# Scatters of normed rows spread over a group, in a kernel of attention and a mixture of experts

## The chip, the cores and the metric

One core of one Trainium2 chip runs the kernel. The metric is the device time of one execution in microseconds. Before the change the median of three runs is 1402.72 us (1402.52 to 1405.96).

## The reference

The input x is 64 sequences of 128 tokens of width 256, float32. Cross attention with 16 heads of 16 is followed by a mixture of 8 experts, of which each token takes two.

```
x = x + attention(layernorm(x), ctx, ctx; Wq,bq,Wk,bk,Wv,bv,Wo,bo)   # 16 heads, softmax over 128 keys
y = layernorm(x)
probs = softmax(y @ router)            # 8 experts
w, idx = top_k(probs, 2); w = softmax(w)
x = x + sum over the 2 chosen e of w_e * (silu(y @ gating[e]) * (y @ up[e])) @ down[e]
```

## The kernel before, in words

**Two parts.** Part one runs over 16 groups (g) of 4 sequences (b = 0 to 3, i = 4g+b). One turn of i is called a stage here. The attention of a sequence is spread over several stages, and beside it the same stages norm the attention's result (x1), choose each token's experts and write the normed rows, sorted by expert, to a table `sorted_x` in device memory. Part two (FFN) takes units of 256 or 128 rows of that table, all of one expert, and adds each result row to the output.

**The order of TensorE in a stage** (`stage_a` of the tensor block) is written out by hand: `scores(i)` (L527, 32 matmul records over 32 rows and 128 columns), `project(i-2)` and `values` or `queries` (L498, 4 records each), `attend(i-1)` (L552, 32 short records), `swap_max(i)` (L533), a product of keys or queries with 512 columns (L498, 4 records) or, in b = 3, the values of the next group, then four swaps of 128 columns (L504 or L568), in b = 0 the router's product (L576, 16 short records), in b = 2 the places (14 tiny products), and `scores_swapped(i)` (L541, 32 short records), after which the next stage's `scores` follow. A float32 product is two matmul records, each with its weight load (PEld).

**What the rows' scatters are.** `write_rows(g, ...)` (L425) on GpSimd (POOL) issues eight indirect DMAs for group g: for each of the 4 sequences and each of the 2 chosen experts, 128 rows of 261 floats go from `xn2` to the rows that `slots_now` names. In the kernel before, group g-3 is written in group g: four scatters in b = 0 and four in b = 1, in the program's order; they follow `route_rows(g-3)` of VectorE (DVE), which computes the slots in b = 0 between `row_maxes` (L1004) and `take_max_off` (L1011). Nothing but the slots' semaphore holds them, so the eight leave one behind the other. In the FFN the last three groups are written behind tiles 0 and 1, 10 and 11, 16 and 17; there `write_pads` (L466) writes the pads and `add_unit` (L459) adds result rows, all by indirect DMAs.

**What else POOL does in a group:** `root2(g-1)` (L411) in b = 1 behind the scatters, `keep_x(g+1)` (L418) behind it and behind the scores of b = 2, `root(g+2)` (L407) in b = 3.

**Buffers and counts.** `xn2` has two rooms of normed rows (g % 2) and `slots_now` one. `second_norm(g)` of ScalarE (ACT) in b = 2 writes a room and waits until the rows of group g-2 have landed; the last step of `route_rows` waits until the rows of group g-1 have landed. All scatters count on one semaphore, `s_scat`.

**SyncE (SP)** loads x and ctx for group g+2 and a block of expert weights (512 KB each), stores x1, and spreads the keys and queries of sequence i+1 over 32-row strips (`spread`, L280). The queries' spread of b = 3 is behind the ctx load in SP's program and needs the last queries product of that stage.

## Time and profile before

| | |
|---|---|
| median of three runs | 1402.72 us |
| the profiled execution | 1408.98 us |
| its span, first to last instruction | 1407.2 us |
| mean granted TensorE clock | 0.943 |
| TensorE busy (matmul) | 1308.4 us, 93% |
| VectorE, ScalarE, GpSimd busy | 645.9, 560.0, 422.8 us |
| scatters of rows L425 | 128, 124.1 us busy on POOL |

[...] Part one ends at about 676 us of the span.

### The profile page before, as it was taken

The page shows a single profiled execution, that of the slowest core. Times are in us where ns is not written, and L with a number is a line of the kernel's source. Part 1 is how long each engine was busy: PE and PEld are TensorE (multiplying, and loading weights), DVE is VectorE, ACT ScalarE, POOL GpSimd, SP SyncE. Part 2 cuts the span into 40 slices and gives each one's busy share as a digit, 9 for nine tenths or more (in the row PEclk, how much of TensorE's full clock was granted, in tenths as well). Part 3 has the DMA queues.
Part 4 walks back from the last instruction along what each step waited for, and adds up shares of the span by engine and source line. Part 5 has one row for each costly group of instructions (what it writes and reads, how often), then busy time and mean ns, then how long its engine had stood idle before and what let it go on. Part 6 is the DMA issues. An engine that isn't in the chain of part 4 may idle for free.

```text
span 1407.2 us, 30663 instructions
## 1 busy us (share of the span) xinstructions
PE 1308.4 (93%) x11214; PEld 1046.7 (74%) x11215; DVE 645.9 (46%) x1762; ACT 560.0 (40%) x924; POOL 422.8 (30%) x354
## 2 busy tenths in 40 slices
PE   6998898888999888997899899999999999999996
PEld 3676666666666666665688788888888888888996
DVE  3775675555675555665433533233232332323332
ACT  3564554444554444543454132222322223222352
POOL 3112322332313323212324632323323223232332
PEclk9998998888988888987999999999999999999999
DMA  4444333334333333222244443333434334343342
GB/s 129 129 114 129 115 114 109 113 103 121 117 116 112 114 101 88 86 62 77 59 64 74 94 61 50 53 49 53 53 49 53 49 53 53 48 54 46 49 52 34
DMA packets 171586, 112.44 MB, mean 80 GB/s; under 512 B 103345, under 2 KB 158641, under 8 KB 171473
## 3 DMA queue, kind: packets, MB, share of 16 engines
q1 hardware_dynamic: 143984, 72.75, 21.2%
q0 software_dynamic: 26400, 37.09, 15.3%
q8 instruction: 76, 1.25, 0.4%
q10 hardware_dynamic: 1088, 1.05, 0.2%
q14 instruction: 38, 0.30, 0.1%
HBM read 48.59 MB, written 45.46 MB: 67 GB/s over the span
## 4 chain that ended last, share of the span: by engine, by line
PE 86%; issue 6%; DVE 3%; DMA 2%; ACT 1%; another core or an unknown queue 1%; SPq 0%; POOL 0%; ACTq 0%; POOLq 0%; DVEq 0%
PE banks L498 65%; PE banks L527 9%; PE banks L541 5%; PE banks L552 4%; DMA heads<-qT 1%; PE banks L533 1%; PE banks L504 1%; DVE row_max L1004 1%; PE banks L568 1%; DMA out<-x_sb,token 1%; PE banks L576 1%; DMA ctxT_sb<-in_ctx 0%; DVE att_rows L1017 0%; DVE q_less L1011 0%
## 5 line engine op out<-in xcount | busy, mean ns | idle before, releaser
L459 POOL DMA_INDIRECT out<-x_sb,token x135 | 210.3, 1558 | 470.8 <-DVE x_sb L1322 413.3
L849 ACT ACTIVATE qT<-banks 128x1024 f32<-128x1024 f32 (+1 forms) x75 | 70.3, 938 | 485.4 <-PE banks L498 437.8
L1309 DVE TENSOR_TENSOR heads<-qT,banks 128x1024 f32<-128x1024 f32 (+1 forms) x75 | 83.5, 1113 | 358.6 <-PE banks L498 338.5
L498 PE MATMUL banks<-down_sb,heads 128*128 x1080 | 245.7, 379 | 0.9 <-DVE x_sb L1322 0.9
L498 PE MATMUL banks<-xnT,probs 128*128 128x256 f32 (+1 forms) x1184 | 240.8, 360 | 5.9 <-issue 5.7
L498 PE MATMUL banks<-xnT,kT 128*128 128x256 f32 (+1 forms) x1216 | 242.7, 357 | 0.0
L1004 DVE TENSOR_REDUCE row_max<-banks 128x16 f32<-128x2048 f32 x64 | 146.7, 2292 | 191.8 <-PE banks L527 191.7
L498 PEld LDWEIGHTS banks<-xnT,probs 128*128 128x128 f32 x1184 | 207.7, 190 | 33.8 <-issue 9.2
L498 PEld LDWEIGHTS banks<-xnT,kT 128*128 128x128 f32 x1216 | 211.8, 190 | 25.5 <-issue 0.4
L498 PEld LDWEIGHTS banks<-down_sb,heads 128*128 128x128 f32 x1080 | 203.7, 190 | 28.9 <-issue 1.9
L843 ACT ACTIVATE probs<-banks 128x512 f32<-128x512 f32 (+1 forms) x192 | 128.1, 740 | 136.6 <-remote 109.3
L527 PE MATMUL banks<-heads 32*128 32x128 f32 x2048 | 130.9, 313 | 54.0 <-issue 46.9
L425 POOL DMA_INDIRECT sorted_x<-xn,slots_now x128 | 124.1, 970 | 145.3 <-DVE slots_now L1103 86.3
L527 PEld LDWEIGHTS banks<-heads 32*128 32x128 f32 x2048 | 100.1, 203 | 82.0 <-issue 78.7
L1322 DVE TENSOR_SCALAR x_sb<-banks,weight 128x256 f32<-128x256 f32 x135 | 59.8, 480 | 121.4 <-PE banks L498 115.6
L541 PE MATMUL banks<-q_less,heads 32*128 32x128 f32 x2048 | 82.6, 289 | 3.4 <-issue 2.9
L498 PE MATMUL banks<-wo_sb,attnT 128*128 128x256 f32 x256 | 84.7, 459 | 0.9 <-DVE attnT L1032 0.7
L552 PEld LDWEIGHTS banks<-probs,v_aug 128*32 128x32 f32 x2048 | 55.2, 115 | 33.9 <-issue 33.1
L541 PEld LDWEIGHTS banks<-q_less,heads 32*128 32x128 f32 x2048 | 67.8, 190 | 16.3 <-issue 14.9
L498 PE MATMUL banks<-wv_sb,ctxT_sb 128*128 128x256 f32 x256 | 76.8, 429 | 0.4 <-ACT probs L843 0.4
L552 PE MATMUL banks<-probs,v_aug 128*32 128x128 f32 x2048 | 73.8, 288 | 3.1 <-ACT probs L843 3.1
L498 PE MATMUL banks<-ctxT_sb,wk_sb 128*128 128x512 f32 x128 | 63.1, 619 | 8.6 <-DMA ctxT_sb<-in_ctx 7.9
(165 smaller groups left out, 1286.1 us busy)
## 6 DMA issues: line engine op xcount, KB each, us to landing
xn<-sorted_x SPq DMA_DIRECT2D x240, 64.0 KB
x_sb<-in_x SPq DMA_DIRECT2D x16, 512.0 KB, 3.8
ctxT_sb<-in_ctx SPq DMA_DIRECT2D x16, 512.0 KB, 4.1
heads<-kT SPq DMA_DIRECT2D x128, 64.0 KB, 2.0
heads<-qT SPq DMA_DIRECT2D x128, 64.0 KB, 2.0
out<-x SPq DMA_DIRECT2D x16, 512.0 KB
gate_sb<-_L_ffn_kernel_gating_EDF SPq DMA_DIRECT2D x8, 512.0 KB
up_sb<-in_L_ffn_kernel_up_EDF SPq DMA_DIRECT2D x8, 512.0 KB
```

Of the source, the lines that this page charges most:

```text
L425: pool.indirect_dma_start(out=sorted_x[:, :], out_offset=bass.IndirectOffsetOnAxis(ap=slots_now[:, i:i + 1], axis=0), in_=xn2[:, u, i % GR ...
L459: pool.indirect_dma_start(out=out[:, :], out_offset=bass.IndirectOffsetOnAxis(ap=token[:, v, h:h + 1], axis=0), in_=ys[:, 2 * u + h, :], i ...
L498: last = nc.tensor.matmul(dst, lhsT, rhs, start=(i == 0), stop=(i == len(pairs) - 1))
L504: last = nc.tensor.transpose(bank[:, b * P:(b + 1) * P], xn[:, b, c * P:(c + 1) * P], ident[:])
L527: last = nc.tensor.matmul(score_banks(i)[:, j, c * TOK:(c + 1) * TOK], q_heads[strip(j), i % 2, c, :], k_heads[strip(j), i % 2, c, :], sta ...
L541: last = nc.tensor.matmul(score_banks(i)[:, j, c * TOK:(c + 1) * TOK], k_heads[strip(j), i % 2, c, :], q_less[strip(j), c, :], start=True, ...
L552: last = nc.tensor.matmul(bank[32 * j:32 * j + 32, q * TOK:(q + 1) * TOK], v_aug[:, i % 3, 4 * q + j, :], probs[:, j, c, :], start=True, s ...
L843: nc.scalar.activation(probs[:, j:j + n].rearrange("p j h t -> p j (h t)"), score_banks(i)[:, j:j + n], ACT.Exp, scale=DK ** -0.5).then_in ...
L849: nc.scalar.activation(gatedT[:, 0:w * F], gate_up[:, 0:w * F], ACT.Silu).then_inc(s_silu, 1)
L1004: nc.vector.reduce_max(row_max[:].rearrange("p (j r a) -> p j r a", r=16, a=2)[:, :, 0:4, 1], score_banks(i).rearrange("p j (h t) -> p j h ...
L1309: nc.vector.tensor_tensor(fusedT[:, u, 0:w * F], gatedT[:, 0:w * F], gate_up[:, 1024:1024 + w * F], ALU.mult).then_inc(s_fuse, 1)
L1322: last = nc.vector.tensor_scalar(ys[:, 2 * u + h, :], work[:, 0, h * D:(h + 1) * D], weight[:, v, h:h + 1], None, ALU.mult)
```

## The change

`xn2` gets three rooms (g % 3), `slots_now` two (g % 2), and the semaphore of the rows becomes one for each room. Group g's scatters are spread over the stages of group g+3 and one of them over b = 0 of g+4, each held by a semaphore of TensorE's: behind "scores of i done" or behind "attend(i-1) done". `keep_x` moves from the end of POOL's b = 1 to the start of its b = 2. `route_rows(g-3)` moves on VectorE from before `take_max_off` to behind `turn_attn` of b = 0. The waits for landed rows are for g-3 (rooms) and g-2 (slots). In the FFN two scatters more (the last two of group 12) stand behind tile 0.

```
+ROOMS = 3
-        xn2 = sb("xn2", [P, 2, GROUP, ROW])
+        xn2 = sb("xn2", [P, ROOMS, GROUP, ROW])
-        slots_now = sb("slots_now", [P, 2 * GROUP], u32)
+        slots_now = sb("slots_now", [P, 2, 2 * GROUP], u32)
+        s_rows_out = [sem(f"rows_written_room{r}") for r in range(ROOMS)]
+        def wait_rows(eng, g):
+            eng.wait_ge(s_rows_out[g % ROOMS], (g // ROOMS + 1) * 2 * GROUP * 16)
...
-            def write_rows(g, u, half, part=(0, GROUP)):
+            def write_rows(g, part):
                 wait(pool, s_route, g * ROUTE_STEPS + ROUTE_STEPS)
                 pool.nop(nofuse=True)
-                for i in range(GROUP * half + part[0], GROUP * half + part[1]):
+                for i in part:
                     pool.indirect_dma_start(
-                        out=sorted_x[:, :], out_offset=bass.IndirectOffsetOnAxis(ap=slots_now[:, i:i + 1], axis=0),
-                        in_=xn2[:, u, i % GROUP, :], in_offset=None).then_inc(s_scat, 16)
+                        out=sorted_x[:, :], out_offset=bass.IndirectOffsetOnAxis(ap=slots_now[:, g % 2, i:i + 1], axis=0),
+                        in_=xn2[:, g % ROOMS, i % GROUP, :], in_offset=None).then_inc(s_rows_out[g % ROOMS], 16)
...
             def stage_a(g, u, core, prev, prev2, prev3, nxt, far):      # POOL
                 for b in range(GROUP):
+                    i = g * GROUP + b
+                    if b == 2 and nxt:
+                        keep_x(g + 1, 1 - u)
+                    if g >= 3:
+                        pool.wait_ge(s_score, i + 1)
+                        if b == 0 and g >= 4:
+                            write_rows(g - 4, (6,))
+                        if b == 1:
+                            write_rows(g - 3, (0, 1))
+                        if b == 3:
+                            write_rows(g - 3, (4,))
+                        pool.wait_ge(s_att, i)
+                        if b == 0 and g >= 4:
+                            write_rows(g - 4, (7,))
+                        if b == 1:
+                            write_rows(g - 3, (2,))
+                        if b == 2:
+                            write_rows(g - 3, (3,))
+                        if b == 3:
+                            write_rows(g - 3, (5,))
+                    if b == 1 and prev:
+                        root2(g - 1)
                     if b == 3 and far:
                         root(g + 2)
-                    if b == 0 and prev3:
-                        write_rows(g - 3, 1 - u, 0)
-                    if b == 1:
-                        if prev3:
-                            write_rows(g - 3, 1 - u, 1)
-                        if prev:
-                            root2(g - 1)
-                        if nxt:
-                            keep_x(g + 1, 1 - u)
...
             def behind_tile(t):                                          # POOL, FFN
+                if t == 0:
+                    write_rows(GROUPS - 4, (6, 7))
...
-            def second_norm(g, u, pieces):
+            def second_norm(g, pieces):
                 wait(act, s_shift2, g + 1)
-                if not isinstance(g, int) or g > 1:
-                    wait(act, s_scat, BLANKS * 16 + (g - 1) * 2 * GROUP * 16)
-                normalise(xn2[:, u], x1, rstd2, shift2, pieces, s_norm2, cut=True)
+                if g >= ROOMS:
+                    wait_rows(act, g - ROOMS)
+                normalise(xn2[:, g % ROOMS], x1, rstd2, shift2, pieces, s_norm2, cut=True)
...
-                if not isinstance(g, int) or g > 0:
-                    wait(dve, s_scat, BLANKS * 16 + g * 2 * GROUP * 16)
-                steps.done(nc.vector.tensor_copy(slots_now[:], slot_f[:]))
+                if g >= 2:
+                    wait_rows(dve, g - 2)
+                steps.done(nc.vector.tensor_copy(slots_now[:, g % 2], slot_f[:]))
...
                     if b == 3 and far:                                   # DVE, stage_a
                         first_stats(g + 2, (2, 3))
-                    if b == 0 and prev3:
-                        route_rows(g - 3, 1 - u)
...
                     if one:
                         turn_attn(i - 1)
+                    if b == 0 and prev3:
+                        route_rows(g - 3)
```

## Rows read from the trace of the kernel before

**Rows 1.** The page: span, busy time of the engines, busy tenths in 40 slices.

```profile
PE 1308.4 (93%) x11214; PEld 1046.7 (74%) x11215; DVE 645.9 (46%) x1762; ACT 560.0 (40%) x924; POOL 422.8 (30%) x354
PEclk9998998888988888987999999999999999999999
```

**Rows 2.** Windows (length; PE, PEld, DVE, ACT, POOL busy; clock; DMA): group 2; last, group 3's b=3.

```profile
86.28:94.21 7.93, 7.93 (x130) 5.75 (x131) 5.13 (x9) 5.99 (x14) 0.00 (x0) 1.00 0.38 101
94.21:101.98 7.77, 7.74 (x115) 5.60 (x116) 6.63 (x21) 4.58 (x11) 1.01 (x1) 1.00 0.34 104
...
109.92:118.62 8.70, 7.81 (x114) 5.39 (x115) 6.94 (x20) 5.75 (x13) 1.02 (x1) 1.00 0.40 105
...
152.68:160.39 7.71, 7.71 (x114) 5.40 (x115) 6.94 (x19) 4.75 (x12) 1.02 (x1) 1.00 0.39 104
```

**Rows 3.** The same windows for b = 0 of the 13 groups 3 to 15.

```profile
118.62:135.45 16.83, 13.06 (x130) 8.91 (x130) 5.97 (x16) 5.01 (x12) 7.82 (x8) 0.78 0.34 105
...
sum 217.99, PE 164.39 PEld 112.18 DVE 78.07 ACT 71.27 POOL 100.88; mean PE 12.65 PEld 8.63 DVE 6.01 ACT 5.48 POOL 7.76
```

**Rows 4.** The same for b = 1 of these 13 groups.

```profile
135.45:144.74 9.29, 9.21 (x115) 6.69 (x116) 6.64 (x21) 4.61 (x11) 1.04 (x1) 0.85 0.29 88
177.19:187.62 10.43, 10.40 (x115) 7.28 (x116) 6.63 (x21) 4.56 (x11) 1.04 (x1) 0.74 0.25 78
...
sum 128.43, PE 127.15 PEld 90.37 DVE 87.74 ACT 58.02 POOL 13.53; mean PE 9.78 PEld 6.95 DVE 6.75 ACT 4.46 POOL 1.04
```

**Rows 5.** POOL's timeline in group 3 (start, length, what, idle before).

```profile
123.17 1.08 POOL L425 DMA_INDIRECT sorted_x<-xn,slots_now  x1 [6.29 <-DVE slots_now L1103]
...
132.17 0.96 POOL L425 DMA_INDIRECT sorted_x<-xn,slots_now  x1 [0.30 <-issue]
142.05 1.04 POOL L411 TENSOR_TENSOR rstd<-var_eps,minus_half 128x4 f32<-128x4 f32 x1 [8.93 <-DVE var_eps L995]
144.87 2.36 POOL L418 TENSOR_TENSOR x_bo<-x_sb,bo_sb 128x1024 f32<-128x1024 f32 x1 [1.78 <-PE banks L527]
```

**Rows 6.** DMA from 120 to 140 us, GB/s in 40 slices of 0.5 us.

```profile
GB/s 29 55 158 379 363 72 0 0 33 167 92 8 267 16 109 159 0 267 0 100 167 0 259 8 67 201 0 251 17 0 0 70 76 117 131 102 29 0 305 350
```

**Rows 7.** PE's timeline of group 3 beside the scatters.

```profile
124.42 1.29 PE L541 MATMUL banks<-q_less,heads 32*128 32x128 f32 x31
...
128.91 1.09 PE L527 MATMUL banks<-heads 32*128 32x128 f32 x5 [0.94 <-issue]
...
134.63 0.78 PE L527 MATMUL banks<-heads 32*128 32x128 f32 x2 [0.35 <-issue]
```

**Rows 8.** Timeline of group 2, without scatters.

```profile
97.29 1.88 PE L498 MATMUL banks<-ctxT_sb,wk_sb 128*128 128x512 f32 x4
...
100.75 1.17 PE L527 MATMUL banks<-heads 32*128 32x128 f32 x32
```

**Rows 9.** Windows: the stretch at the lower clock in group 3.

```profile
128.10:138.30 10.20, 7.47 (x27) 5.54 (x28) 2.63 (x3) 2.00 (x3) 3.84 (x4) 0.50 0.28 91
```

**Rows 10.** Timeline of the FFN: PE and POOL where 20 indirect DMAs follow closely.

```profile
784.01 0.99 POOL L425 DMA_INDIRECT sorted_x<-xn,slots_now  x1 [0.30 <-issue]
...
788.45 7.07 PE L498 MATMUL banks<-xnT,kT 128*128 128x256 f32 x32
...
800.37 1.91 PE L498 MATMUL banks<-xnT,probs 128*128 128x256 f32 x6 [1.40 <-issue]
802.60 1.12 PE L498 MATMUL banks<-xnT,probs 128*128 128x256 f32 x4 [0.33 <-issue]
804.03 1.11 PE L498 MATMUL banks<-xnT,probs 128*128 128x256 f32 x4 [0.31 <-issue]
```

**Rows 11.** The chain of waits at the end of group 2 (start, length, what).

```profile
113.88 3.37 DMA heads<-qT
```

**Rows 12.** Timeline of b = 0 of group 3: VectorE and the swap.

```profile
121.17 0.17 DVE L1093 TENSOR_SCALAR total<-gap 128x4 f32<-128x4 f32 x1
...
122.20 0.74 DVE L1011 TENSOR_TENSOR q_less<-heads,banks 128x256 f32<-128x256 f32 x2
...
123.31 0.60 PE L504 MATMUL banks<-ident,xn 128*128 128x128 f32 x4
```

91 lines of the change are left out of this document (47 added, 44 removed).

## The prediction

> **What bounds the kernel now.** I read the page first, then the timeline around the scatters, then windows cut from one row maximum to the next (one stage each), then the chain. The page says that TensorE is busy 93% of the span [rows 1], which seems to leave nothing. But a busy TensorE can be a slow one: its granted clock is 9 tenths or more in the slices of the FFN and falls to 8 or 7 in many of part one [rows 1]. The windows show where. Group 2, which writes no rows yet, has its b = 0 and b = 1 in 7.93 and 7.77 us, TensorE busy throughout at clock 1.00 [rows 2]. In the 13 groups that write rows, b = 0 takes 217.99 us together, 16.8 each [rows 3], and b = 1 128.43, some 9.9 each [rows 4]. The number of matmul records of the two is the same as in group 2 (130 and 115), so this is no added work of TensorE.
>
> The timeline says what it is. Eight scatters leave POOL from 123.17 to 133.13, one each 1.27 us [rows 5]. DMA traffic of theirs begins 1.3 to 1.8 us behind the first issue and ends by 134.5 [rows 6]. Beside it the scores product L527, which needs 1.17 us for 32 records without scatters [rows 8], comes in handfuls with "issue" idle time between, until 135.4 [rows 7]: TensorE waits for no semaphore, its instructions come late. [...]
>
> The FFN shows the same thing beside longer products. POOL issues 20 indirect DMAs from 784.01 on. TensorE's 256-column records go at full pace (32 in 7.07) until 798.97, then they too come in fours: one batch at 802.60, the next at 804.03, 1.43 us apart [rows 10]. So I take it thus: while scatters are in flight TensorE is fed some 4 records with their loads in 1.43 us, and it lives on a store of instructions. Size of the store: from 785.5 (issue plus 1.5) to 798.97 it ran 13.5 / 0.22 = 61 records (0.22 = 7.07 / 32) and was fed 13.5 / 1.43 x 4 = 38, so the store held about 23. A 512-column record takes 1.88 / 4 = 0.45 us or so [rows 8], 3 in 1.43 us: such a product does not need the store at all. The short ones use 39 in that time.
>
> **Ceiling.** Removing all the excess: b = 0, 217.99 - 13 x 7.93 = 114.9; b = 1, 128.43 - 13 x 7.77 = 27.4; together 142.3 us [rows 2 to 4]. The profiled execution took 1408.98 us (span 1407.2, 1.8 around it), so 1266.7. It stands 6.3 us above the median of 1402.72; for the median the ceiling is 1260.4. As that difference is small beside 142.3, the excess is there in unprofiled runs too, and no matter of the recording.
>
> **The change part by part.** Time is counted from the end of a stage's scores; behind it come two products (to 1.9), attend (to 2.9), the row maximum's swap, the 512-column product (to 4.9), swaps of 128 columns, scores_swapped and the next scores, to 7.8 or so. A scatter starts 0.9 us behind its releaser (slots ready at 122.28, POOL at 123.17 [rows 5, 12]) and its traffic some 1.5 behind that.
>
> Held by the scores (number 6 in b = 0, 0 and 1 in b = 1, 4 in b = 3): traffic from 2.4, beside the row maximum's swap and the long product. The long product keeps its pace; what is left is attend's tail and the swap, whose instruction may come late. Ends: 0, and 1.10, what a scatter costs in today's b = 0 (114.9 / 104). I take 0.3, near the long products' row.
>
> Held by attend (7 in b = 0, 2 in b = 1, 3 in b = 2, 5 in b = 3): released at 2.9, traffic from 5.3. That is not the long product, it is scores_swapped and the next scores, 64 short records. One pause of 1.43 us [rows 10] against a store of some 23 short records at 0.037 us (0.9 us) leaves 0.5. Ends again 0 and 1.10. The first train bears it out: beside its first two scatters L541 ran 31 records in 1.29 us [rows 7], against 1.17 for 32 short ones undisturbed [rows 8], the full stops came later.
>
> In b = 1 three follow closely (2.4, 3.7, 5.3): a lean stretch of some 4.3 us, in which 12 records are fed; the swaps, the long product and the xn swaps take about 10 of them, so scores_swapped finds the store nearly empty. I take 1.3 for the three, ends 0 and 3.3.
>
> In b = 3 the queries' spread is a chain of its own: in group 2 the scores waited for that DMA, 3.37 us, behind the ctx load [rows 11], and the stage took 8.70 instead of 7.71 [rows 2]. Two scatters now move data beside it: ends 0 and 1.0, I take 0.2 here.
>
> Sum per group: b = 0, 0.3 + 0.5; b = 1, 1.3; b = 2, 0.5; b = 3, 0.3 + 0.5 + 0.2; 3.6 us. Group 3 has no b = 0 part: 2.8. So 12 x 3.6 + 2.8 = 46.0. With all at the low ends 0; with all scatters at today's price 102 x 1.10 + 13 = 125.
>
> The clock: stalls of under 1.5 us with dense work between are what group 2's own 0.99 us wait was, and the clock stayed 1.00 there [rows 2]. I take 27.4 as saved whole.
>
> At nothing I put: route_rows behind turn_attn (today it delays the subtraction to 122.20, yet the xn swap starts at 123.31 right behind the long product [rows 12]; VectorE is busy 5.13 of the 7.93 us of a b = 0 without it [rows 2], and the idle rest holds its 1.1 us; if that cover is gone the next row maximum starts up to 1.1 us late). The waits for rooms and slots: rows land 2 us behind issue and are waited for two or more stages later. keep_x: today it already starts with the scores of b = 2, at 144.87, not with the end of b = 1 [rows 5]; SP's load of x hangs on it and stays. root2 is behind scatter 2 in POOL's order, over by 4.8; its input comes at about 6.5 (8.93 us of idle before 142.05 [rows 5]). root: input later still. Behind POOL's new waits stand only these. The two scatters more behind tile 0 lie beside records that kept full pace for 13 us [rows 10]; ends 0 and 2.2.
>
> [...]
>
> [...]
>
> **Sum.** 1266.7 + 46.0 = 1312.7 in the profile's terms, less 6.3: 1306.4. I forecast 1306.
>
> **Rivals.**
> 1. The store covers a lone scatter whole. For it: the first two of the train cost next to nothing [rows 7]. Against: the pause, 1.43, is longer than the store lasts with short products. Cost 0 to 1.3 a group, so 1260 to 1277; say 1270. Chance 0.17.
> 2. A scatter costs the same wherever it is, and only the clock comes back: 104 scatters at 1.10 are kept. 1402.7 - 27.4 = 1375. Against: FFN products at full pace [rows 10]. Chance 0.08.
> 3. [...] Group 2 has the same loads and stores without the loss, so 0.02.
> 4. Slower: the clock. Today one train costs one stretch of 10.2 us at 0.50 [rows 9], worth about 2.1 us of b = 1 plus its part in b = 0. Thin spots in all four stages could bring it down several times a group. A stretch in which TensorE has full work loses half of 10.2, 5.1 us. With three stretches a group and the stalls of 3.6: 18.9 instead of 10.9 today (142.3 / 13), 8 more for 13 groups, 1507; it decides from about 1.5 stretches a group ((10.9 - 3.6) / 5.1 = 1.4). Against: group 2. Chance 0.04.
>
> The forecast, partial return, has 0.69. Its own range: 1278 to 1350 (cost 1.4 to 7 a group). The whole range, to hold 8 in 10, reaches down to rival 1 and not quite to rival 2: 1264 to 1350. A difference of 0.3% is about what a measurement of this kernel can tell from none. Faster 0.93, the same 0.02, slower 0.05 (rival 4 and what I don't see).
>
> **What would show it.** Right: b = 0 windows of 8 to 9.5 us, clock 1.00 in groups 3 to 14; scatters at 0.9 us behind their releasers; "issue" idle time before L541 and L527 of up to 1.4 us a time, in b = 1 most, and little before L498. Wrong on the placing: stalls before the swap L533 or in L552, which would put the cost on the scatters held by the scores. Wrong on b = 3: L527 waiting for the heads' DMA in most groups. Wrong altogether: windows with clock 0.50 in part one beyond its last group, or stages over 12 us.

## The result and the profile after

| | before | after |
|---|---|---|
| median, us (range, 4 runs each) | 1402.62 (1402.41 to 1405.96) | 1274.86 (1274.27 to 1275.91) |
| ratio, 95% interval | | 0.9079 (0.9062 to 0.9096) |
| profiled execution, us; its span | 1408.98; 1407.2 | 1274.27; 1272.5 |
| b = 0 of groups 3 to 14, mean us | 16.80 | 7.94 |
| b = 1 / b = 2 / b = 3, mean us | 9.88 / 7.98 / 8.13 | 8.22 / 7.84 / 8.11 |
| part one at the lower clock, us | 153.6 | 6.8 |
| from the last row maximum to the end, us | 739.5 | 744.6 |

The change returned 127.8 us, on the chip where this pair was timed; on two others it returned nothing, as the experiments show. The forecast of 1306 expected 96.6; 1274.9 lies in the range, but below the 1278 at which the forecast's own range begins, among the numbers of rival 1 (1260 to 1277). The row numbers of the source move: the scores' product is L551 now (L527 before), scores_swapped L565 (L541), the swap L557, the 512-column and 256-column product L522 (L498), the scatters L434 (L425).

The page of the kernel after, the lines that answer to [rows 1]: TensorE's busy share rises because its time falls less than the span.

```profile
PE 1221.5 (96%) x11214; PEld 991.1 (78%) x11215; DVE 645.8 (51%) x1762; ACT 561.3 (44%) x924; POOL 424.4 (33%) x354
PEclk9999999999999999899999999999999999999999
```

Windows of the kernel after, from row maximum to row maximum (columns as in [rows 2]; a clock of 1.00 is the full speed of TensorE granted throughout, 0.50 half of it). First b = 0 of groups 3 and 5 with the sum over groups 3 to 14, against [rows 3]: group 5 has two scatters beside it (2.00 us of POOL) and takes 7.93 us, what group 2 takes without any [rows 2].

```profile
116.32:124.25 7.93, 7.93 (x130) 5.75 (x131) 6.03 (x16) 4.97 (x12) 0.00 (x0) 1.00 0.30 86
179.29:187.22 7.93, 7.93 (x130) 5.75 (x131) 6.04 (x16) 5.99 (x14) 2.00 (x2) 1.00 0.47 136
...
sum 95.31, PE 95.31 PEld 69.18 DVE 72.44 ACT 68.56 POOL 22.00; mean PE 7.94 PEld 5.77 DVE 6.04 ACT 5.71 POOL 1.83
```

Then b = 1 of groups 5 and 10 and the sum, against [rows 4]: 8.00 with three scatters and clock 1.00, and one outlier of 10.26, whose VectorE is busy for 8.58 instead of 6.55 us.

```profile
187.22:195.22 8.00, 7.95 (x115) 5.54 (x116) 6.55 (x21) 4.67 (x11) 3.93 (x4) 1.00 0.47 152
345.37:355.63 10.26, 10.25 (x146) 7.47 (x150) 8.58 (x21) 5.44 (x11) 6.23 (x5) 1.00 0.47 144
...
sum 98.67, PE 97.98 PEld 69.79 DVE 80.59 ACT 56.81 POOL 49.86; mean PE 8.17 PEld 5.82 DVE 6.72 ACT 4.73 POOL 4.15
```

The timeline of the kernel after in b = 0 of group 5 (start, length, what, idle before it), against [rows 7]. Scatters leave POOL at 180.08 and 183.01. Both short products run whole, 32 records in 1.17 and 1.09 us, and ScalarE's exponential of the scores starts 0.34 us behind the start of L565's last record (185.99). The second scatter's data moved from 184.55 to 184.90, beside the swaps.

```profile
180.08 1.03 POOL L434 DMA_INDIRECT sorted_x<-xn,slots_now  x1 [1.50 <-PE banks L551]
...
183.01 0.97 POOL L434 DMA_INDIRECT sorted_x<-xn,slots_now  x1 [1.90 <-PE banks L576]
...
185.09 1.17 PE L565 MATMUL banks<-q_less,heads 32*128 32x128 f32 x32
...
186.08 1.09 PE L551 MATMUL banks<-heads 32*128 32x128 f32 x32
186.33 2.00 ACT L867 ACTIVATE probs<-banks 128x512 f32<-128x512 f32 x3 [0.80 <-PE banks L565]
```

Where the 134.7 us between the two profiled spans went: the stages from group 3 to the last row maximum 137.5 (b = 0 114.2, b = 1 19.9, the rest 3.4), the part ahead of group 3 2.3, and 5.1 lost again behind the last row maximum. The profiled execution of before stood 6.3 us above its median, that of after 0.6 below it, so 127.8 by the medians.

The trace of before says more than the prediction took from [rows 7]. In the timeline of group 3 of the kernel before, L541's last record starts at 125.97; the exponential that waits for it starts 8.69 us later.

```profile
125.97 0.34 PE L541 MATMUL banks<-q_less,heads 32*128 32x128 f32 x1 [0.27 <-issue]
...
134.66 2.00 ACT L843 ACTIVATE probs<-banks 128x512 f32<-128x512 f32 x3 [8.43 <-remote]
134.70 1.10 SPq L280 DMA_DIRECT2D heads<-kT  x2
```

It starts when the train is over (POOL's last scatter ends at 133.13), and SP's spread with it. In the stages without scatters beside it that distance is 0.34 to 0.48 us. So TensorE was not only fed late: what waits for it learned late that it was done. Below, this is called the hold.

### The profile page after: what moved, and what is told of

Read it like the earlier page. It is cut to its first block, busy times and chain, and to the rows that moved or that the text cites. A ratio compares the mean times of both kernels' runs of the same rounds, so it can differ in the third digit from the quotient of the medians.

```text
span 1272.5 us, 30742 instructions
## 1 busy us (share of the span) xinstructions
PE 1221.5 (96%) x11214; PEld 991.1 (78%) x11215; DVE 645.8 (51%) x1762; ACT 561.3 (44%) x924; POOL 424.4 (33%) x354
## 3 DMA queue, kind: packets, MB, share of 16 engines
q10 hardware_dynamic: 1088, 1.05, 0.3%
## 4 chain that ended last, share of the span: by engine, by line
PE 89%; DVE 4%; DMA 2%; issue 2%; ACT 1%; SPq 0%; POOL 0%; another core or an unknown queue 0%; ACTq 0%; POOLq 0%; DVEq 0%
PE banks L522 71%; PE banks L551 5%; PE banks L565 4%; PE banks L576 4%; DVE row_max L1028 1%; PE banks L528 1%; PE banks L557 1%; DMA heads<-qT 1%; PE banks L592 1%; DMA out<-x_sb,token 1%; PE banks L600 1%; DVE att_rows L1041 1%; DVE q_less L1035 1%; DMA ctxT_sb<-in_ctx 0%; PE banks L606 0%
## 5 line engine op out<-in xcount | busy, mean ns | idle before, releaser
L1333 DVE TENSOR_TENSOR heads<-qT,banks 128x1024 f32<-128x1024 f32 (+1 forms) x75 | 83.5, 1113 | 356.7 <-PE banks L522 338.8
L522 PE MATMUL banks<-xnT,probs 128*128 128x256 f32 (+1 forms) x1184 | 242.7, 361 | 4.4 <-issue 4.4
L522 PE MATMUL banks<-down_sb,heads 128*128 x1080 | 245.5, 379 | 1.2 <-DVE x_sb L1346 0.9
L522 PE MATMUL banks<-xnT,kT 128*128 128x256 f32 (+1 forms) x1216 | 244.8, 359 | 0.0
L522 PEld LDWEIGHTS banks<-xnT,probs 128*128 128x128 f32 x1184 | 208.6, 191 | 32.9 <-issue 7.9
L522 PEld LDWEIGHTS banks<-xnT,kT 128*128 128x128 f32 x1216 | 213.1, 192 | 26.6 <-issue 1.0
L522 PEld LDWEIGHTS banks<-down_sb,heads 128*128 128x128 f32 x1080 | 204.0, 190 | 29.2 <-issue 2.2
L434 POOL DMA_INDIRECT sorted_x<-xn,slots_now x128 | 125.2, 978 | 251.5 <-PE banks L551 139.6
L551 PE MATMUL banks<-heads 32*128 32x128 f32 x2048 | 75.0, 283 | 6.7 <-DMA heads<-qT 4.8
L576 PEld LDWEIGHTS banks<-probs,v_aug 128*32 128x32 f32 x2048 | 52.7, 110 | 31.9 <-issue 31.3
L565 PE MATMUL banks<-q_less,heads 32*128 32x128 f32 x2048 | 76.0, 285 | 1.1 <-DVE q_less L1035 1.1
L551 PEld LDWEIGHTS banks<-heads 32*128 32x128 f32 x2048 | 65.3, 189 | 12.9 <-issue 8.8
L576 PE MATMUL banks<-probs,v_aug 128*32 128x128 f32 x2048 | 70.0, 278 | 4.5 <-ACT probs L867 4.5
L522 PE MATMUL banks<-wo_sb,attnT 128*128 128x256 f32 x256 | 73.2, 409 | 0.7 <-DVE attnT L1056 0.7
L565 PEld LDWEIGHTS banks<-q_less,heads 32*128 32x128 f32 x2048 | 63.7, 188 | 11.7 <-issue 9.7
L522 PE MATMUL banks<-ctxT_sb,wk_sb 128*128 128x512 f32 x128 | 61.9, 608 | 8.3 <-DMA ctxT_sb<-in_ctx 7.8
L522 PE MATMUL banks<-wv_sb,ctxT_sb 128*128 128x256 f32 x256 | 66.0, 380 | 0.4 <-ACT probs L867 0.4
```

The lines of the kernel that those rows point to most:

```text
L434: pool.indirect_dma_start(out=sorted_x[:, :], out_offset=bass.IndirectOffsetOnAxis(ap=slots_now[:, g % 2, i:i + 1], axis=0), in_=xn2[:, g ...
L522: last = nc.tensor.matmul(dst, lhsT, rhs, start=(i == 0), stop=(i == len(pairs) - 1))
L551: last = nc.tensor.matmul(score_banks(i)[:, j, c * TOK:(c + 1) * TOK], q_heads[strip(j), i % 2, c, :], k_heads[strip(j), i % 2, c, :], sta ...
L565: last = nc.tensor.matmul(score_banks(i)[:, j, c * TOK:(c + 1) * TOK], k_heads[strip(j), i % 2, c, :], q_less[strip(j), c, :], start=True, ...
L576: last = nc.tensor.matmul(bank[32 * j:32 * j + 32, q * TOK:(q + 1) * TOK], v_aug[:, i % 3, 4 * q + j, :], probs[:, j, c, :], start=True, s ...
L1333: nc.vector.tensor_tensor(fusedT[:, u, 0:w * F], gatedT[:, 0:w * F], gate_up[:, 1024:1024 + w * F], ALU.mult).then_inc(s_fuse, 1)
```

## The experiments

Two theories stand in the texts of the first four kernels, both taken from the prediction. S: scatters that follow one another empty TensorE's store of instructions, so the length of the train decides, and one or two cost nearly nothing. P: what decides is which product lies beside the traffic; beside short ones each scatter costs 1.1 us, beside long ones nothing. The store is my estimate from [rows 7, 8, 10]; no run shows it by itself. The first four kernels ran on one chip, where the kernel before took 1411.18 us (1408.41 to 1411.88). All change the kernel after.

**e1: the three rooms, but the old train of eight, and keep_x in its old place.**

```diff
-                        if b == 0 and g >= 4: write_rows(g - 4, (6,))   # and all other places
+                    if b == 0 and g >= 3:
+                        write_rows(g - 3, range(2 * GROUP))
...
+                    if b == 1 and nxt:
+                        keep_x(g + 1, 1 - u)                            # and not at the start of b = 2
```

> All of the change but the spreading: three rooms, two slots, route_rows moved on VectorE, but POOL issues the eight scatters of a group one behind the other in b = 0, held by nothing but the slots. Theory S (a store of TensorE's instructions is emptied by scatters that follow one another): b = 0 windows again about 16.8 us and b = 1 about 9.9, 1395 to 1405 us. Rival R (the rooms, slots or the move of route_rows carry part of the gain): under 1385 us.

Measured 1394.65 us, ratio 0.9889 (0.9873 to 0.9906); at the scale of the result's chip 1387. Rooms and route_rows' place together are worth one per cent, part of it perhaps because the train now starts later; the other eight come from the spreading, with keep_x's move, which no run has by itself. The time lies just under S's 1395 and over the 1385 of the rival; the timeline says more. The train starts at 164.66, late in b = 0, and runs into b = 1 (mean stages 9.51 and 15.74). The last swap is issued at 169.46, and VectorE, which waits for it, starts 7 us later; ScalarE waits for the 512-column product, whose records end at 171.89, and starts 4.7 us behind that. Both start behind the train (POOL's last start is 173.58):

```profile
169.16 0.41 DVE L1043 SCALAR_TENSOR_TENSOR x<-banks,x_bo 128x256 f32<-128x256 f32 x1
...
169.46 0.27 PE L589 MATMUL banks<-ident,logitsT 128*128 128x128 f32 x1
...
169.61 0.39 SPq L296 DMA_DIRECT2D out<-x  x1
169.62 0.51 ACT L812 ACTIVATE squares<-x,x_sum 128x256 f32<-128x256 f32 x1 [1.49 <-issue]
...
173.58 0.96 POOL L434 DMA_INDIRECT sorted_x<-xn,slots_now  x1 [0.30 <-issue]
176.50 0.75 DVE L1018 TENSOR_TENSOR q_less<-heads,banks 128x256 f32<-128x256 f32 x2 [6.92 <-remote]
176.54 0.69 ACT L838 ACTIVATE kT<-banks,bk_sb 128x512 f32<-128x512 f32 x1 [6.33 <-remote]
```

In the middle of the train VectorE's x reaches SP and ScalarE at once (its record ends at 169.57, they start at 169.61 and 169.62). So it is TensorE's word that is late, not everybody's; the counts under the last heading bear that out.

**e2: two trains of four, held by the scores in b = 1 and b = 3.**

```diff
-                    if g >= 3:
+                    if g >= 3 and b in (1, 3):
                         pool.wait_ge(s_score, i + 1)
-                        pool.wait_ge(s_att, i)                          # and the eight single places
+                        write_rows(g - 3, range(0, 4) if b == 1 else range(4, 8))
```

> The changed kernel with four scatters in a row behind the scores of b = 1 and four behind those of b = 3. Theory S: the store carries about three pauses beside a mixed stage, so each train of four costs 1 to 2 us: 2 to 4 us a group, 1300 to 1325 us, clock mostly 1.00. Theory P (what counts is which product lies beside the traffic; short ones cost 1.1 us a scatter): the traffic of a train reaches from 2.4 to 6.8 us behind the scores, half of it beside short products, 4 x 1.1 a group: 1330 us.

Measured 1368.97 us, 0.9702 (0.9683 to 0.9721): far more than either theory gave. Stages b = 1 12.04 and b = 3 11.23. Here the train begins at 206.71, ahead of attend (207.72), so the swap falls into it: product at 208.90, its reader at 212.61, 1.06 us behind the end of the last scatter (211.55). Neither theory has this wait.

```profile
208.90 0.27 PE L590 MATMUL banks<-ident,logitsT 128*128 128x128 f32 x1
...
210.59 0.96 POOL L434 DMA_INDIRECT sorted_x<-xn,slots_now  x1 [0.30 <-issue]
212.61 0.75 DVE L1019 TENSOR_TENSOR q_less<-heads,banks 128x256 f32<-128x256 f32 x2 [4.06 <-remote]
```

**e3: one train of eight behind the scores of b = 1.**

```diff
-                    if g >= 3:
+                    if g >= 3 and b == 1:
                         pool.wait_ge(s_score, i + 1)
-                        if b == 0 and g >= 4: write_rows(g - 4, (6,))   # and all other places
+                        write_rows(g - 3, range(0, 8))
```

> The changed kernel with all eight scatters in a row behind the scores of b = 1, so that the first meet the long product. Theory S: the length of the train decides, so nearly as slow as before: 1370 to 1400 us, with one stretch at clock 0.50 a group. Theory P: the two or three scatters beside the long product are free, 5 to 6 cost 1.1 us, and less clock loss: 1340 to 1360 us.

Measured 1385.8 us, 0.9824 (0.9775 to 0.9874). b = 1 takes 15.59 us, b = 2 8.88; 122.9 us at the lower clock. The four runs lie 14 us apart (1377.31 to 1391.62). All of them are far above P's 1360 and inside S's range, so P is out. But the number fits a TensorE whose readers hear late as well as a store that runs dry: between these two it is not decisive.

**e4: pairs, each held by attend, so that they fall on the short products.**

```diff
-                        pool.wait_ge(s_score, i + 1)                    # and its single scatters
                         pool.wait_ge(s_att, i)
                         if b == 0 and g >= 4:
-                            write_rows(g - 4, (7,))
+                            write_rows(g - 4, (6, 7))
+                        if b > 0:
+                            write_rows(g - 3, (2 * b - 2, 2 * b - 1))
```

> The changed kernel with none of the scatters held by the scores: two in a row behind attend of every stage, so that their traffic (5.3 to 7 us behind the scores) lies on scores_swapped and the next scores, the short products. Theory S: two pauses in a row fit the store, so about the time of the changed kernel, 1272 to 1285 us. Theory P: eight scatters at 1.1 us beside short products, 13 groups: 1370 to 1390 us. The sum of the prediction (0.5 us each) would give 1310 to 1330 us.

Measured 1296.21 us, 0.9184 (0.9169 to 0.9199), 1288 at the result's scale, 1.05% of before above the kernel after. Stages 8.50, 7.77, 8.79, 8.54, clock 1.00 but for 13.7 us. The placing that puts every scatter's data beside scores_swapped and the scores costs 1.7 us a group over the undisturbed stages (33.6 against 31.9 us), for eight scatters. It lies 11 us above S's range (1272 to 1285; 3 us at the result's scale), far below P's 1370, and below the 1310 to 1330 of the prediction's sum: eight scatters at 0.5 would lose 4 us a group. That fells the prediction's price; nor does S's "nearly nothing" for pairs hold.

**p1 and p2: kinds and lengths of trains, in groups 1 and 2, which have no scatters of their own.** They write blanks to a scratch tensor.

```diff
+                    if g == 1 and b == 0:
+                        pool.wait_ge(s_score, i + 1); spill_train(0, "indirect", 8)      # p2: 2 of them
+                    if g == 1 and b == 2:
+                        spill_train(8, "direct", 8)                                      # p2: 3 indirect
+                    if g == 2 and b == 0:
+                        pool.wait_ge(s_score, i + 1); spill_train(16, "indirect thin", 8)  # p2: 4 indirect
+                    if g == 2 and b == 2:
+                        spill_train(24, "direct thin", 8)                                # p2: 6 indirect
```

> The changed kernel with four extra trains of eight POOL DMAs each into tables that nothing reads, placed in groups 1 and 2, which write no rows: b = 0 of group 1, indirect, 128 rows of 1044 bytes (the control); b = 2 of group 1, direct DMAs of the same bytes; b = 0 of group 2, indirect, 128 rows of 16 bytes; b = 2 of group 2, direct, 16 bytes a row. What is read is the time from TensorE's last scores_swapped record to ScalarE's exponential (0.34 us undisturbed, 8.5 in the old train) and the length of the stage. Theory T (making the descriptors of an indirect DMA on POOL holds TensorE's signals): both indirect trains hold them alike, 7 us or more, the direct ones don't. Rival B (the bytes moved by the software queue do it): the first two hold them, the thin ones don't. Rival D (any software DMA): all four.

> The changed kernel with extra trains of indirect scatters of full rows into a table that nothing reads, of 2 (b = 0 of group 1), 3 (b = 2 of group 1), 4 (b = 0 of group 2) and 6 (b = 2 of group 2), one behind the other. Theory T (signals are held while scatters follow one another, and a gap frees them): the loss grows from under 0.5 us at 2 through some 0.5 at 3, 3 to 4 at 4, to over 6 at 6. The store of instructions alone (prediction) would give 0.5, 1.3, 2.4 and 5.

Neither told the indirect kinds or the lengths apart, since this set ran on another chip, and there the effect is all but missing. The kernel before took 1261.8 us (1259.18 to 1263.78, 17 runs) on it, p1 1262.36, p2 1260.68 (a single run each). p2's stages with two, three, four and six scatters take 7.66, 7.66, 7.93 and 8.04 us. p1's train of direct DMAs (b = 2 of group 1) did cost something even here: in b = 3 the scores wait 1.79 us for the heads' DMA, the stage takes 9.62 in place of some 7.8 us, and the next, beside the thin train, 9.61 with 3.4 us at clock 0.50. That is a loss through the DMA, not through TensorE's word. Two more kernels of that set show no gain either.

**after_again (the kernel after, unchanged) and i1 (an attempt to mend what it still lost).** i1 puts two scatters into every stage (after has 2, 3, 1 and 2), one behind the scores and one behind attend, in b = 2 behind the queries less their maximum; it lets keep_x wait for VectorE's second shift, and spreads the eight scatters of each of the last two groups over three tiles in place of two:

```diff
                     if b == 2 and nxt:
+                        wait(pool, s_shift2, g)
                         keep_x(g + 1, 1 - u)
...
+                        if b > 0: write_rows(g - 3, (2 * b - 2,))
+                        if b == 2: pool.wait_ge(s_less, i * 2 + 2)
+                        else: pool.wait_ge(s_att, i)
+                        if b > 0: write_rows(g - 3, (2 * b - 1,))
...
-                if t in (10, 11): write_rows(GROUPS - 2, range(GROUP * (t - 10), GROUP * (t - 9)))
+                if t in (10, 12, 14): k = (t - 10) // 2 * 3; write_rows(GROUPS - 2, range(k, min(k + 3, 2 * GROUP)))
```

(16, 17 likewise become 16, 18, 20, and the pads' 18, 19 become 22, 24.)

> The changed kernel itself, for comparison with the next on the same chip: ratio 0.908 to the kernel before.

> The changed kernel with the rest of its trains taken apart. Part one: no two scatters directly behind one another (numbers 0, 2, 4, 6 behind the scores, 1, 3, 5, 7 behind attend, in b = 2 behind the queries less their maximum); the 8.00 us of b = 1 should fall to 7.77: 3 us. keep_x waits for the shift of the second norm, which it held up by 2 us in one group. FFN: three scatters a unit instead of eight, pads behind tiles 22 and 24, where eight and eight followed one another: the 4.7 us of idle TensorE there go. Sum 8 to 10 us less than the changed kernel, ratio 0.901 to 0.903 to the kernel before. Rival: these waits lie beside others and it stays within 3 us of the changed kernel.

On this chip the kernel after took 1261.01 us, ratio 0.9996 (0.9987 to 1.0005): no difference at all. i1 took 1266.05, 1.0024 (1.0013 to 1.0035). So the change is worth 9.2% on one chip and nothing on another, and it is the kernel before that differs, by 141 us; the kernel after differs by 14.

**p4: the kinds again, on a chip that shows the effect** (the kernel before took 1405.24 us there). Eight direct DMAs in group 0 b = 2, then eight indirect, four indirect 2.3 us apart, eight indirect of 16-byte rows, eight indirect of 32 rows.

```diff
+                    if g == 0 and b == 2: spill_train(0, "direct", 8)
+                    if g == 1 and b == 0: pool.wait_ge(s_score, i + 1); spill_train(8, "indirect", 8)
+                    if g == 1 and b == 2: spill_train(16, "indirect", 4, P, 1)
+                    if g == 2 and b == 0: pool.wait_ge(s_score, i + 1); spill_train(24, "indirect thin", 8)
+                    if g == 2 and b == 2: spill_train(32, "indirect", 8, 32)
```

> In the set before, the kernel before the change took 1261.8 us, as the changed one did, and trains of eight held nothing: the loss depends on the chip. So this run is read with the time of the kernel before beside it. The changed kernel with five extra trains into tables that nothing reads, in the groups that write no rows: b = 2 of group 0, eight direct DMAs of 128 x 1044 bytes; b = 0 of group 1, eight indirect of the same (control); b = 2 of group 1, four indirect 2.3 us apart; b = 0 of group 2, eight indirect of 128 x 16 bytes; b = 2 of group 2, eight indirect of 32 rows. On a chip where the kernel before takes about 1400 us, the control stage should grow by 6 to 9 us. Theory T (making descriptors for indirect DMAs holds TensorE's signals): the thin train costs as much, the direct one nothing, the spaced one under 1 us. Rival B (bytes): direct as much as the control, thin nothing. On a chip where the kernel before takes about 1262 us: all stages under 8.8 us.

1308.28 us, a single run. Windows of p4: the stages with eight indirect, with four spaced, with eight thin, with eight of 32 rows, and the one behind the last.

```profile
58.44:72.75 14.31, 11.57 (x114) 8.22 (x114) 5.13 (x10) 5.03 (x10) 7.83 (x8) 0.74 0.33 117
...
82.42:91.22 8.80, 8.38 (x116) 5.89 (x117) 5.12 (x9) 6.38 (x11) 8.02 (x7) 1.00 0.64 195
98.83:114.71 15.88, 10.66 (x130) 7.79 (x131) 5.13 (x9) 6.75 (x14) 7.73 (x8) 0.79 0.27 56
122.50:139.61 17.11, 12.36 (x128) 8.72 (x128) 6.52 (x19) 6.48 (x12) 9.31 (x9) 0.76 0.35 101
139.61:149.15 9.54, 8.89 (x114) 6.18 (x115) 6.94 (x20) 4.57 (x10) 1.04 (x1) 0.89 0.30 78
```

Against the same stages undisturbed: +6.7 for eight full ones (and 2.0 more in the stage behind), +1.1 for four with gaps, +8.0 for eight whose rows are 16 bytes, +9.2 for eight of 32 rows. Fewer bytes or rows don't make it cheaper. That the gaps do is less clean, as the spaced train also has four in place of eight; but e2's close trains of four cost 4.3 and 3.1 us (12.04 and 11.23 against 7.77 and 8.11). The eight direct ones of group 0 fell on b = 3, 10.24 instead of 7.33 us. That +2.9 is no measure of the hold: 2.15 us of it are TensorE's wait for the heads' DMA, as in p1 on the chip without the effect, and none of TensorE's signals is late there. (Group 1's b = 0 without trains takes 7.66; the others 7.7 to 8.0.)

In the train of eight full ones the signals are late, but do not all wait for its end. The row maximum's swap is issued at 61.95, and its reader starts 2.99 us later in place of 0.37, between scatters that follow without a gap:

```profile
61.95 0.33 PE L590 MATMUL banks<-ident,row_max 128*128 128x128 f32 x1
...
64.46 0.96 POOL L429 DMA_INDIRECT spill<-blank,spill_rows  x1 [0.31 <-issue]
64.94 0.75 DVE L1068 TENSOR_TENSOR q_less<-heads,banks 128x256 f32<-128x256 f32 x2 [3.88 <-remote]
```

The same train stands in p1 too, with the same products beside it. In windows of p1, on the chip without the effect, that stage takes 8.20 us, TensorE at clock 1.00:

```profile
52.72:60.92 8.20, 8.16 (x116) 5.97 (x117) 5.13 (x9) 6.39 (x13) 5.87 (x6) 1.00 0.61 181
```

and in its timeline the exponential, 0.34 us behind the start of its product's last record, starts in the midst of the train:

```profile
58.73 0.96 POOL L429 DMA_INDIRECT spill<-blank,spill_rows  x1 [0.30 <-issue]
59.18 2.00 ACT L898 ACTIVATE probs<-banks 128x512 f32<-128x512 f32 x3 [0.39 <-PE banks L596]
59.99 0.96 POOL L429 DMA_INDIRECT spill<-blank,spill_rows  x1 [0.30 <-issue]
```

One scatter each 1.27 us, 0.96 long, in p1 and in p4 (medians 1.265 and 1.264): POOL's records are alike, TensorE's side differs. The 0.54 us that p1's stage has over 7.66 are one late signal, that of the scores beside the scatter of 59.99 (0.57 us), the only one of that trace's part one.

**i1_again: the same kernel as i1, beside p4.**

> The same kernel as before without scatters directly behind one another. On a chip where the kernel before takes about 1400 us: 9 us less in the FFN (units 6, 9 and 10 of the changed kernel took 13.5, 17.4 and 11.7 us against 10.8, 11.8 and 8.9 on the other chip), 3 in b = 1, and 4 more in POOL's last DRAIN (6.7 instead of 2.6 us): 8 us less than the changed kernel, ratio about 0.902. On a chip where the kernel before takes 1262 us: 1.002 again.

Measured 1283.46 us, 0.9135 (0.912 to 0.915); expected was 0.902. Its b = 2 takes 9.23 us in the mean where the kernel after takes 7.84. There, and nowhere else in the part, a scatter leaves POOL 0.15 us ahead of the row maximum's swap; POOL comes to it straight from keep_x, without a wait. Timeline of i1 on this chip, b = 2 of group 5:

```profile
202.47 1.03 POOL L434 DMA_INDIRECT sorted_x<-xn,slots_now  x1 [0.17 <-issue]
202.62 0.33 PE L557 MATMUL banks<-ident,row_max 128*128 128x128 f32 x1
...
203.99 0.75 DVE L1035 TENSOR_TENSOR q_less<-heads,banks 128x256 f32<-128x256 f32 x2 [0.96 <-PE banks L557]
```

The same place, kernel and order on the chip without the effect (0.46 us from swap to reader in place of 1.37):

```profile
198.93 1.03 POOL L434 DMA_INDIRECT sorted_x<-xn,slots_now  x1 [0.16 <-issue]
199.07 0.33 PE L557 MATMUL banks<-ident,row_max 128*128 128x128 f32 x1
199.53 0.75 DVE L1035 TENSOR_TENSOR q_less<-heads,banks 128x256 f32<-128x256 f32 x2
```

It is so in all 12 groups (1.26 to 1.37 us from swap to reader). This is the clearest of the pairs: one scatter, no train, no starved product, the clock at 1.00, and the reader is late by 0.9 us, until 0.5 us behind POOL's record. The miss against 0.902, 16 us, is this: 12 x 1.39 = 16.7 us. p4's spaced four are the same case: the first follows keep_x by 0.16 us and the swap falls on it, and that signal's 0.86 us are most of their 1.1.

i1's other edit did what it should. VectorE's fuse (L1333) ends a unit of the FFN. In the timeline of the kernel after, units of 17.42 and 11.72 us:

```profile
650.33 1.22 DVE L1333 TENSOR_TENSOR heads<-qT,banks 128x1024 f32<-128x1024 f32 x1 [0.29 <-PE banks L522]
667.75 1.22 DVE L1333 TENSOR_TENSOR heads<-qT,banks 128x1024 f32<-128x1024 f32 x1 [5.61 <-remote]
679.47 1.18 DVE L1333 TENSOR_TENSOR heads<-qT,banks 128x1024 f32<-128x1024 f32 x1
```

and in that of i1 on this chip the same two take 11.64 and 9.05. Over the three units hit (13.5, 17.42, 11.72 against 10.77, 11.64, 9.05) the kernel after loses 11.2 us to its trains of scatters and pads. The units right behind are shorter than in i1 (9.89 and 8.91 against 10.47 and 10.36) and give 2.0 back, so the net loss is 9.2 us.

**after_beside_i3 and i3: the kernel after with only the FFN's spread and keep_x's wait.** Its diff is i1's without the middle part.

> The changed kernel once more, to stand beside the next one on the same chip. If the kernel before takes about 1402 to 1411 us here (its b = 0 stages 16.8 us): ratio 0.908, stages of part one 7.9, 8.0 to 8.2, 7.8, 8.1 us for b = 0 to 3, the FFN's units behind tiles 10 and 16 some 9 us together longer than on the chip that shows no loss. If the kernel before takes about 1261 us: ratio 1.000 and no such 9 us.

> The changed kernel with two edits: the last two groups' scatters go 3, 3 and 2 behind tiles 10, 12, 14 and 16, 18, 20 in place of 4 and 4 behind 10, 11 and 16, 17 (the pads behind 22 and 24 in place of 18 and 19), and POOL's keep_x waits for VectorE's second shift. Theory A (TensorE's signals and supply are held up while POOL makes descriptors without a gap; trains in the FFN cost what the former spread kernel got back there): where the kernel before takes 1402 to 1411 us, the units behind tiles 10 and 16 come back to 10.8 and 11.6 us, 9 us less than in the changed kernel; group 10's 2.1 us of two-input subtraction beside keep_x comes down to 0.16 and returns up to 2 us; if POOL's last DRAIN takes 6.7 us again in place of 2.6, 4 of it are lost at the end. Together 7 to 11 us: ratio 0.900 to 0.903. Theory B (the FFN's loss is a matter of the neighbours of each scatter, not of the train): ratio unchanged, 0.907 to 0.909. Where the kernel before takes 1261 us: 0.998 to 1.003 by both.

These ran on one more chip, where the kernel before takes 1262.19 us (1260.14 to 1264.49, 19 runs). After 0.9994 (0.9984 to 1.0003), i3 1.0023 (1.0012 to 1.0033). So the chip of p1 was no exception, and i3's gain where the effect exists is not measured. By the 9.2 us of the FFN, 2 of the outlier below, and 4 lost at the end, some 7 us of 1275 could be had; that is an estimate. i1_again bears out its larger part: from the last row maximum to the end it takes 739.8 us against 744.6.

## Why the prediction came out as it did

**The ceiling was right to 6%.** It said 142.3 us in b = 0 and b = 1 of part one; 134.1 came back there, and 3.4 in b = 2 and b = 3, for which it had nothing: 137.5. In the profile's terms the sum was 1266.7 + 46.0 = 1312.7; measured 1274.3. From the ceiling to the measured time: 1266.7, + 4.8 that the stages of part one keep, - 2.3 ahead of group 3, + 5.1 behind the last row maximum = 1274.3.

**The step that failed is the price of a scatter alone, "cost 0.3 + 0.5" and the like, 3.6 us a group.** Measured against the undisturbed ones: b = 0 0.0 in place of 0.8; b = 1 0.23 in the median in place of 1.3; b = 2 and b = 3 nothing (7.84 and 8.11, below or at before's 7.98 and 8.13) in place of 0.5 and 1.0. Some 3 us in all, not 46. The two bounds that I had written down, 0 and 1.10, were the right ones; I took the middle by a mechanism that the rows bore out only in part. That 1274.9 lies in the whole range is owed to its low end, which rival 1 had set, and to the chip: on two others the same pair has a ratio of 1.00, which nothing in the prediction foresaw.

**The mechanism was misread.** "TensorE waits for no semaphore, its instructions come late" is true of its own idle time [rows 7], and the picture of a store fed four records in 1.43 us, an estimate, fitted the FFN [rows 10] (where 18 indirect DMAs follow from 784.01 on, not 20). It left out the other half, that what waits for TensorE hears late of it. With the store alone, placing scatters under long products was the cure. With the hold, what decides in these runs is whether TensorE ends something that an engine waits for while scatters that follow other work of POOL without a wait are being made. The kernel after avoids that in most places, though it was not placed for it: its scatters are single and start 0.8 us behind attend or the scores, but for two that follow directly in b = 1. Three answers bear it out: e4, which has pairs in every stage and loses 1.7 us a group; i1, whose scatter stands on the signal, right behind keep_x, and loses 1.39; p4, whose close eight lose 6.7 to 9.2. A scatter that POOL has waited for is mostly harmless even when a signal falls into it (49 of 49 on time in the kernel after, 12 late by 0.5 us in i1_again), as the next paragraph shows.

**The b = 1 rest.** Its second scatter follows the first directly and starts 0.8 us ahead of the swap (189.26, 190.03). The reader L1035 starts 1.00 us behind the swap in nearly all 12 groups; the same kernel on the chip of after_again has 0.48 at that place. Price 0.23 a stage. The prediction had b = 1 as its dearest stage, rightly, for another reason. The third scatter shows the other side, in the same timeline: the 512-column product ends at 192.19 in the midst of it, and its reader starts 0.04 us later, on time.

```profile
190.31 1.88 PE L522 MATMUL banks<-ctxT_sb,wk_sb 128*128 128x512 f32 x4
...
191.71 0.96 POOL L434 DMA_INDIRECT sorted_x<-xn,slots_now  x1 [1.48 <-PE banks L576]
...
192.23 0.69 ACT L855 ACTIVATE kT<-banks,bk_sb 128x512 f32<-128x512 f32 x1 [1.74 <-issue]
```

**b = 3.** "A chain of its own", 0.2 us for the heads' DMA: the stage stands at 8.11, no longer than before.

**The clock.** "I take 27.4 as saved whole": 19.9 in b = 1's sum. The 27.4 are b = 1's excess, which I put down to the clock: the stretch at 0.50 of group 3 lasts until 138.30 [rows 9], 2.85 us into b = 1 [rows 4]. Of the 7.5 that are missing, 2.3 are the outlier and 2.1 group 15's b = 1, which also took 9.84 before. Half-clock time went from 153.6 to 6.8 us; rival 4 did not occur. It followed the idle time in every kernel of the first set (99.0, 75.1, 122.9, 13.7 us for e1 to e4), so I take it for a second loss, not a cause; no run changed it by itself.

**The FFN.** "The two scatters more behind tile 0 lie beside records that kept full pace" was wrong, and its upper end of 2.2 us was too low. 4.3 of the 5.1 us lost behind the last row maximum are lost there, ahead of the first unit's end. In the kernel after, the two (532.13 and 533.40) follow a scatter of b = 3 directly, and the scores_swapped product ends at 533.13 beside them. ScalarE's exponential starts at 535.26, 2.1 us later, and TensorE waits for it; then the clock is 0.50 from 536.81 to 543.63.

```profile
533.40 0.96 POOL L434 DMA_INDIRECT sorted_x<-xn,slots_now  x1 [0.30 <-issue]
...
535.26 2.00 ACT L867 ACTIVATE probs<-banks 128x512 f32<-128x512 f32 x3 [1.31 <-remote]
...
537.62 1.93 PE L576 MATMUL banks<-probs,v_aug 128*32 128x128 f32 x32 [4.49 <-ACT probs L867]
539.48 9.21 PE L522 MATMUL banks<-xnT,kT 128*128 128x256 f32 x32
```

(L576 and L522 as TensorE's timeline has them alone.) The same two products in the kernel before:

```profile
675.98 1.08 PE L552 MATMUL banks<-probs,v_aug 128*32 128x128 f32 x32 [3.06 <-ACT probs L843]
676.99 7.17 PE L498 MATMUL banks<-xnT,kT 128*128 128x256 f32 x32
```

1.43 of wait, 0.85 and 2.04 of slower records make the 4.3; on the chip without the effect the same kernel has 1.6 of them. The trains behind tiles 10 and 16, which stay trains, cost nearly what they cost before (the six units there 71.8 us against 71.1). From the last row maximum to the end the kernel after takes 744.6 us here and 732.7 on the chip without the effect.

**The adjustment to the median.** "Less 6.3": the profiled execution of before lay above its median, that of after did not (1274.27 against 1274.86). Carrying before's difference over made 6.3 us of error in the hopeful direction, which the price of the scatters hid.

**The rivals.** Rival 1 gave the right size, 1260 to 1277, and I gave it 0.17. Its text asked the right question (does a lone scatter cost?), its "against" rested on the pause of 1.43 us, which occurs within trains only. Rival 2 (a scatter costs the same wherever it is, 1375) is out by 100 us. Rival 3 deserves a second look.

**Rival 3 again.** That the scatters are not the cause, 1402.7 us, had 0.02. On two chips the runs come near to it: the kernel before at 1262 us, and in p1 8.20 us in place of 7.66 beside eight indirect DMAs, clock 1.00. On the chips of e1 to e4 and of p4, and where the result was measured, the same kernel before takes 11 to 12% longer beside the same DMAs. Whether the traffic slows a TensorE record itself these traces cannot tell, as the ends of its records are modelled. What they show late is its supply ("issue" idle time of 0.26 to 0.94 us in group 3 of the kernel before [rows 7]) and its word (8.69 us in place of 0.34).

**What stays open.** Which part of a scatter does it: POOL's record of 0.96 to 1.03 us, or the data that move behind it. The expectations call what POOL does there the making of descriptors; no trace shows what the record holds, so that is a guess of mine. i1_again speaks against the data. The swap's signal of group 5 is held from 202.95 to 203.91, and from 202.5 to 206.5 POOL's DMA queue moves no packet; the data of that scatter and the next move together, from 206.97 on, 4.5 us behind the issue (in the kernel after, and in the trains, it is about 1.5 us). So POOL's record is enough, with no packet of that queue moving; by which path it reaches TensorE, no run shows. The hold ends 0.5 us behind POOL's record in i1 (203.50, 203.99) and 1.1 to 2.0 us behind the last one in trains (211.55, 212.61; 174.54, 176.50), which is not explained either. Why TensorE, but not VectorE, is held (e1, 169.61) is open. And so is why some chips show it: each chip was used in one set of runs only, so a state of that session is as possible a cause as the chip itself.

## What to carry to other kernels

When TensorE's products come in handfuls with idle time that no semaphore explains, look at the readers too: the distance from a product's last record to the engine that waits for it, beside the same distance elsewhere in the trace, told here in one subtraction (0.34 against 8.69 us) what the idle time alone did not. Don't let POOL issue indirect DMAs back to back, or straight behind other work of its own, beside products that an engine waits for; hold each by a semaphore of TensorE's, so that POOL waits before it. Here eight in a row cost a stage 6.7 to 9.2 us (p4), one straight behind keep_x 1.39 (i1_again), and the two held ones of b = 0 nothing (7.94 us in the kernel after, 7.93 without any [rows 2]). That holds for places outside the busy part too: the two scatters that were thought free behind tile 0 cost most of the 5.1 us. And time both kernels on more than one chip before a change of this kind is called a gain: here it is worth 9% where the result was measured and nothing on two other chips, and costs nothing where it gives nothing.

## What the runs showed of the hardware

The dependence on the chip, or on the session. The kernel before took 1402.62 us (4 runs, the result), 1411.18 (7 runs, beside e1 to e4), 1261.80 (17, beside p1 to i1), 1405.24 (7, beside p4) and 1262.19 (19, beside i3); within a set its runs lie 0.25 to 0.36% apart. POOL's records do not tell the two kinds apart: scatters that follow one another are 0.96 us long and start 1.265 us apart in the traces of the kernel before and e1, 1.264 in p4, 1.265 in after_again, p1 and p2 (medians).

TensorE's signals, counted. A trace has the time of each update of a semaphore and the end of each record that makes one. In part one of the kernel before, 26 of the 540 updates of TensorE's that can be matched to their record come more than 0.2 us behind its end, the others 0.06 us at most. The latest is 8.4 us behind, in group 10; that of L541's record shown above, which ends at 126.31, is at 134.64, 8.3 us behind, and the exponential starts at 134.66. Of VectorE's 951 and ScalarE's 500 the latest is 0.012 us behind. In e1 it is 87 of 546, in the kernel after 40 of 496, the latest 1.05 us, and on the chip of after_again 0 of 546, none over 0.06 us. Of the 40, 39 come behind a scatter that follows another directly. Of the 49 updates that fall into a scatter for which POOL had waited, none is late. That is no strict rule: in i1_again 12 such updates, one a group, are 0.5 us late, and in e1 12, beside the first scatter of the train, 0.38 to 1.99 us.

VectorE's second shift beside POOL's keep_x. In the timeline of the kernel after, group 10, keep_x starts 0.28 us ahead of the second shift (L1023), which then takes 2.09 us in place of 0.16 and ends with it; it is the 10.26 us stage above, and the row maximum behind it waits.

```profile
353.33 2.36 POOL L427 TENSOR_TENSOR x_bo<-x_sb,bo_sb 128x1024 f32<-128x1024 f32 x1 [0.95 <-DVE total L1083]
...
353.61 2.09 DVE L1023 SCALAR_TENSOR_TENSOR shift<-x_sum,rstd 128x4 f32<-128x4 f32 x1
355.63 2.28 DVE L1028 TENSOR_REDUCE row_max<-banks 128x16 f32<-128x2048 f32 x1
```

The other 15 second shifts of the run have no keep_x beside them and take 0.13 to 0.17 us. The prediction placed keep_x "at nothing", and in 11 of 12 groups it was so. Why the two end together, no run shows.

The end of the program: in i1 (on both kinds of chip) and i3 the record of POOL's last DRAIN takes 6.69 us in place of 2.56, 4.1 more. In i3's timeline the last scatter of the output starts at 1252.18 and the span ends at 1263.2; in the kernel after on the same chip 1252.79 and 1259.5. That is as much as i3 takes longer (1265.24 against 1261.13, 0.3%). What makes it is not known.
